# Wait placement and step order redrawn in an attention and state-space kernel on one Trainium2 core

## What is computed

```
# block 1: attention with one head of 128 channels
h = group_norm(x)                                  # 8 groups
q, k, v = split(h @ qkv_w.T + qkv_b)
attn = softmax(q @ k.T / sqrt(128))                # 1024 x 1024 for each image
x = x + (attn @ v) @ proj_w.T + proj_b

# block 2: a selective state-space layer (mamba2) over the 1024 tokens
u = layer_norm(x) * norm_g + norm_b
z, xBC, dt = split(u @ in_w.T);  dt = softplus(dt + dt_bias)
xBC = silu(causal_conv1d(xBC, 4 taps) + conv_b)    # 256 channels: xs 128, B 64, C 64
state = state * exp(dt * A) + dt * xs * B          # 4 heads, from token to token
y = C . state + Dp * xs;  y = rms_norm(y * silu(z)) * rms_w
out = y @ out_w.T
x = x + out * sigmoid(se2(relu(se1(mean_over_tokens(out)))))
```

## Time and profile before

| | us |
|---|---|
| median of 3 runs | 293.25 |
| lowest and highest run | 291.04, 295.36 |
| span of the profiled execution | 289.1 |
| PE busy in it | 262.4 (91%) |
| DVE busy | 238.4 (82%) |
| ACT busy | 210.1 (73%) |
| POOL busy | 113.3 (39%) |

### The profile page before, as it was taken

How to read it: one execution, slowest core, us unless ns; L and a number is a source line. 1 busy time by engine, 2 the same in 40 slices (tenths; PEclk the granted TensorE clock), 3 DMA queues, 4 the chain that set the end, 5 groups by cost and what they waited for, 6 DMA issues and landing times. The chain is left out here.

```text
span 289.1 us, 6193 instructions
## 1 busy us (share of the span) xinstructions
PE 262.4 (91%) x1992; PEld 224.1 (78%) x1992; DVE 238.4 (82%) x517; ACT 210.1 (73%) x414; POOL 113.3 (39%) x114
## 2 busy tenths in 40 slices
PE   3999999999999999989899997899899996999691
PEld 2889978888887788778888696787898885576581
DVE  5795767447869899899999999989998998797933
ACT  2346678968999758859868974877587967888260
POOL 7000043152055201196454172333751166756171
PEclk9999999999999999999999999999999999999995
DMA  5920000040004400000265000330007100000013
GB/s 160 409 101 2 0 2 1 6 144 0 2 0 130 96 0 2 0 2 1 73 161 140 0 2 0 105 83 2 0 6 194 63 1 2 36 0 3 0 39 146
DMA packets 10987, 15.29 MB, mean 53 GB/s; under 512 B 1515, under 2 KB 5708, under 8 KB 10956
## 3 DMA queue, kind: packets, MB, share of 16 engines
q1 hardware_dynamic: 10412, 14.69, 16.3%
q10 hardware_dynamic: 544, 0.21, 0.3%
HBM read 12.70 MB, written 2.20 MB: 52 GB/s over the span
## 5 line engine op out<-in xcount | busy, mean ns | idle before, releaser
L1157 PEld LDWEIGHTS attn_out<-values,pT 128*128 128x128 f32 x512 | 62.1, 191 | 5.8 <-issue 4.5
L1157 PE MATMUL attn_out<-values,pT 128*128 128x129 f32 x512 | 65.5, 275 | 0.3 <-DVE res L985 0.3
L974 DVE TENSOR_REDUCE neg_max<-scores 128x1 f32<-128x1024 f32 x32 | 39.0, 1219 | 11.9 <-PE scores L1157 11.7
L649 ACT ACTIVATE probs<-scores,neg_max 128x512 f32<-128x512 f32 x64 | 41.6, 684 | 9.1 <-DVE neg_max L974 7.8
L655 ACT ACTIVATE pT<-turn 128x512 f32<-128x512 f32 x64 | 37.5, 594 | 11.3 <-PE turn L1230 11.0
L1230 PE MATMUL turn<-ident,probs 128*128 128x128 f32 x256 | 37.4, 274 | 1.7 <-ACT pT L655 1.7
L575 POOL TENSOR_TENSOR pre<-pre,th 128x512 f32<-128x512 f32 x16 | 22.0, 1373 | 42.6 <-ACT pre L681 39.6
L1230 PEld LDWEIGHTS turn<-ident,probs 128*128 128x128 f32 x256 | 29.9, 142 | 5.6 <-issue 3.5
L561 POOL TENSOR_TENSOR ln_rstd<-ln_var,neg_half 128x4 f32<-128x4 f32 x8 | 11.4, 1430 | 55.7 <-DVE ln_var L996 55.6
L1067 DVE TENSOR_TENSOR_SCAN L<-L,ident 128x512 f32<-128x512 f32 x24 | 28.9, 1219 | 0.7 <-DMA L<-decay_rows_d 0.7
L1157 PE MATMUL scores<-h_hi,q_hi 128*128 128x512 f32 x64 | 28.2, 441 | 0.6 <-DVE q_lo L970 0.6
(11 more groups left out here) (219 smaller groups left out, 606.4 us busy)
## 6 DMA issues: line engine op xcount, KB each, us to landing
L<-decay_rows_d SPq DMA_DIRECT2D x24, 256.0 KB, 3.9
res<-in_x_tok SPq DMA_DIRECT2D x4, 512.0 KB, 8.1
out<-res SPq DMA_DIRECT2D x8, 256.0 KB, 2.1
x_all<-in_x SPq DMA_DIRECT2D x3, 512.0 KB, 8.4
decay_in<-decay_rows_d SPq DMA_DIRECT2D x24, 64.0 KB, 3.6
x_all<-in_x SPq DMA_DIRECT2D x2, 256.0 KB, 3.1
winT<-in_in_wT SPq DMA_DIRECT2D x1, 194.0 KB, 6.9
wqkv<-in_qkv_w ACTq DMA_DIRECT2D x1, 192.0 KB, 4.0
```

The source lines that it names most:

```text
L649: act.activation(probs[:, i % 2, half_of(h)], scores[:, half_of(h)], ACT.Exp, bias=neg_max[:, i:i + 1]).then_inc(exp_done.sem, 1)
L974: V.tensor_reduce(neg_max[:, n:n + 1], scores[:, :], AX.X, ALU.max, negate=True).then_inc(max_ready.sem, 1)
L1157: return T.matmul(o, w, v, start=start, stop=stop)
```

## The change

Two things change and nothing else. No instruction is added or taken away on any engine, and the number of EVENT_SEMAPHORE instructions on each engine stays.

First, in the code of some 45 kinds of steps the `wait` calls are written in another order, so that another one of them stands on the instruction. In many cases `take(...)`, which waits for PE's filling of the bank, is now first.

Second, ORDER is a new table, with new bank numbers.

```diff
@@ act: step pT
                     i, h = divmod(n, 2)
+                    bank = take(act, b, "T", n)
                     wait(act, pv_done, b, n - 3)
-                    bank = take(act, b, "T", n)
@@ pool: step g
+                    wait(pool, y_ready, b, n + 1)
                     wait(pool, gate_ready, b, n + 1)
-                    wait(pool, y_ready, b, n + 1)
@@ pe: step S
-                    wait(pe, q_lo_ready, b, i // QUAD + 1)
-                    wait_h_lo(pe, b, h + 1)
                     if i == 0:
                         wait(pe, q_lo_ready, b, h + 1)
                     else:
                         wait(pe, exp_done, b, n - 1)
+                    wait(pe, q_lo_ready, b, i // QUAD + 1)
+                    wait_h_lo(pe, b, h + 1)
@@ pe: step T
+                    wait(pe, exp_done, b, n + 1)
                     pe.wait_ge(vp_ready.sem, 1)
-                    wait(pe, exp_done, b, n + 1)
                     bank, done = fill(pe, b, "T", n)
@@ pe: step PV
+                    if h == 0:
+                        wait(pe, res_ready, b, i)
                     wait(pe, pT_ready, b, n + 1)
                     wait(pe, v_ready, b, h + 1)
-                    if h == 0:
-                        wait(pe, res_ready, b, i)
@@ pe: step UT
+                    wait(pe, u_tok_ready, b, n + 1)
                     pe.wait_ge(win_ready.sem, 1)
                     pe.wait_ge(gn_var_ready.sem, 2)
-                    wait(pe, u_tok_ready, b, n + 1)
@@ ORDER, its first row before and now
-gn_stats0 warm3 gn_mm10 kq_mm gn_dev0 gn_mm20 vp_mm gn_ve0 kq_ev gn_pow0 gn_aff0 h0a h_hi0a h1a h_hi1a h_lo0a h_lo1a
+warm3 gn_stats0 gn_mm10 kq_mm gn_dev0 gn_mm20 kq_ev gn_ve0 vp_mm gn_pow0 gn_aff0 h0a h1a warm5 h_hi0a h_hi1a h_lo0a
```

More of the change, by code:

```diff
@@ new lines @@
+h_lo1a Q0a vp_ev Q1a win_s q_hi0a q_lo0a alog V0a@1 S0a q_hi1a q_lo1a v0a S1a gn_bs1 max0a exp0a xob0b gn_bs2 win_mm
+V1a@0 T0a@1 exp1a S2a v1a xob0a pT0a S3a T1a@0 max1a gn_bs3 pT1a PV0a PV1a exp2a S4a exp3a inv0a T2a@1 S5a res0a pT2a
+stats0a T3a@0 max2a pT3a PV2a exp4a PV3a exp5a S6a T4a@1 pT4a S7a T5a@0 inv1a gn_stats1 res1a gn_mm11 PV4a max3a pT5a
+stats1a win_ev gn_dev1 PV5a exp6a exp7a inv2a S8a res2a T6a@0 S9a max4a T7a@1 pT6a pT7a exp8a PV6a xob1b stats2a PV7a
+T8a@1 inv3a res3a stats3a exp9a S10a pT8a T9a@0 ln_ve0a S11a wo_s PV8a max5a gn_mm21 pT9a gn_ve1 ln_pow0a PV9a gn_pow1
@@ new lines @@
+g1b o0b stats0d XsT0c@0 UT1c@1 PV3d pT5d T6d@0 T7d@1 bc3c u1c Dt1c@2 exp8d sq1b InBC1c@1 xdt0c dt_x1c l3c exp9d
+sp_exp1c os0b pT6d to_end0c xend0c InX1c@0 sp9c fin0a S10d inv1d raw_bc1c Ss1b@2 res1d pT7d sp10c ms1b T8d@1 term3c
+term4c sp11c dd0c raw_x1c S11d sp12c conv_bc4c sp13c sp14c conv_x4c U0c@1 Out1b@2 PV4d st0c G0c@0 y_pow1b sp15c
+stats1d sp16c PV5d max5d o1b sp17c exp10d Cum1c@1 S12d dA1c m0c os1b inv2d dec1c res2d stc0c m1c pT8d conv_bc5c cd1c
+conv_x5c exp11d PV6d term5c DAT1c@2 stats2d PV7d m2c T9d@0 inv3d InZ1c@1 conv_bc6c rows1c conv_bc7c conv_x6c zt1c
@@ L1055, in step @@
                     rows = slice(R * n, R * (n + 1))
+                    bank = take(dve, b, "XsT", n)
                     wait(dve, sp_step, b, SP_STEPS * n + SP_DT)
@@ L1093, in step @@
                     part = slice(P, HALF) if n == 0 else half
+                    bank = take(dve, b, "Yo", n)
                     if by_dma(b):
@@ L1099, in step @@
                     wait(dve, xs_ready, b, n + 1)
-                    bank = take(dve, b, "Yo", n)
                     V.tensor_tensor(yo[:, part], bank[:, P if n == 0 else 0:HALF], decay_in[:, part], ALU.mult
@@ L1117, in step @@
                 elif kind == "y":
+                    bank = take(dve, b, "Y", n)
                     wait(dve, yo_dx_ready, b, n + 1)
@@ L1362, in step @@
                 elif kind == "Pl":
-                    bank, done = fill(pe, b, "Pl", n)
                     if b < BATCH - 1:
@@ L1370, in step @@
                         tiles = [o_tok[:, QUAD * n + k, :] for k in range(QUAD)]
+                    bank, done = fill(pe, b, "Pl", n)
                     for k, t in enumerate(tiles):
```

195 lines of the change are left out of this document (96 added, 99 removed).

## The result

| | before | changed |
|---|---|---|
| median, us | 293.35 (4 runs, 291.0 to 295.4) | 275.91 (4 runs, 275.3 to 276.2) |
| ratio to before, 95% interval | | 0.942 (0.936 to 0.948) |
| span of the profiled execution | 289.1 | 273.1 |
| PE busy | 262.4 (91%) | 256.9 (94%) |
| DVE busy | 238.4 (82%) | 224.8 (82%) |

The kernel is 17.4 us faster. Some executions of a kernel are slower as a whole, at a lower granted clock, so times and ratios from here on are of the fast ones. The prediction was 290.0 us with a range from 284.8 to 295.5, so it was wrong: right in sign, five times too small, and outside its own range. The number that it named as a test of itself is the one that moved most after the span: DVE is shown busy 13.6 us less, with the same instructions.

A forecast was written before the change was run, and what follows sets the result against it. PE was taken to bound until 90 us, DVE until 241 us, then a chain across engines. From the 289.1 us span, 1.9 and 1.5 us off and 0.2 added gave 285.9, hence a median of 290.0 us, range 284.8 to 295.5.

The forecast's parts named there:

- What bounds the kernel: PE bounds from 14.8 to 90 us, DVE by a hair to 241 us, then a chain that hops between engines.
- Part one: Hops whose late wait moves onto the instruction get shorter on PE, ACT and POOL: 1.9 us gained (0.7 to 3.9).
- Part two: The new order covers long stalls, mostly in the DVE-bound stretch: 1.5 us gained, less 0.2 us at the head.
- three stalls that I looked up: Cum1c's 1.19 us wait for `la`, Out1a's 1.44 us for its bank, SP's 0.41 us store issue: 3.0 us.
- the weight of two fifths for PE's time: In the DVE-bound stretch, PE's 2.6 us of removed stalls were counted at two fifths, 1.1 us.
- The head: First 14.8 us: order kept but for three edits; ACT's alog stands in the way of q_lo1a, costing 0.2 us.
- The end: From the last `la` of the attention part on, nine hops from UT1d to the last th_att save 0.7 us.
- the last rival: DVE operations held while POOL works meet it more often, each losing 0.5 to 1.1 us: slower, chance 0.16.
- The waits bite deeper: Shorter hops in the attention loop and half of DVE's idle time closed: 7.7 us gained, about 285 us, chance 0.27.
- Nothing: DVE's work from 90 to 241 us stays, hiding PE's stalls; only the end's 0.7 us gained: 292.5 us, chance 0.15.
- The tests: Signs in the later profile: shorter hops, stalls gone, end 0.7 us shorter, DVE's busy time of 238.4 within 3 us.

The follow-up runs named there:

- before_memset: The kernel before with each large POOL operation replaced by memsets of its target that read no SBUF operand: 279.09 us, ratio 0.957.
- without holding: Large POOL operations replaced by memsets that read no SBUF operand: kernel before 279.1 us, with new waits 278.5, with new table 274.9, changed kernel 273.0.
- the halves: Against the kernel before, each half of the change alone: new wait order with old table 292.59 us (1.000), new table with old wait order 278.85 us (0.954).

## Why the prediction was wrong, step by step

**What bounds the kernel.** Here it failed first. I read "DVE busy 143.4 of 151.0 us" as 143.4 us of work and took 7.6 us as the most that an order could free. The sum had no term for a change in the number of meetings: it stood at nothing. But 17.3 us of these 143.4 were holding (20 of the 29 held operations lie in that stretch), and having fewer of them is worth some 10 us of the 17.4. The mark of it stood in the earlier trace rows, medians and means far from the minimum, and in the earlier trace rows; I used them for a rival only and never summed them over all lines. A sum of 22.6 us would have put the lower bound of the time some 13 us lower, by the price that before_memset gave.

**Part one, the waits, 1.9 us.** The hops behave as forecast. In the changed trace the S steps that waited for exp start 0.05 to 0.06 us behind it (0.11 to 0.12 before); y ends at 223.24 and POOL's g starts 0.07 us later; ln_var ends at 228.90 and POOL starts 0.08 later; u_tok ends at 231.74 and UT1d starts 0.05 later (0.21 before):

```profile
222.56 0.68 DVE L1122 TENSOR_TENSOR y<-mamba,th 128x512 f32<-128x512 f32 x1
223.31 1.27 POOL L588 TENSOR_TENSOR xs<-y,gate 128x512 f32<-128x512 f32 x1
...
230.46 1.28 ACT L662 ACTIVATE u_tok<-res,ln_rstd 128x128 f32<-128x128 f32 x4 [0.39 <-POOL ln_rstd L561]
231.79 0.42 PEld L1248 LDWEIGHTS mamba<-ident,u_tok 128*128 128x128 f32 x4
```

Their worth was 0 with the old table and 2.9 us with the new one (0.6 and 1.9 without holding), around the 1.9 that I wrote. The size of this term was fair, but about 1 us of the 2.9, and 0.7 of the 1.9, may be the pace of the first Q steps and not the waits.

**Part two, the order, 1.5 us.** This term was mis-sized. The table alone gave 13.4 us. The single readings came true: the stalls of Out1a and Cum1c are gone, and so is the wait of a scan of L for its DMA. What failed is (a) that the new table was credited with three stalls that I looked up, one of which was itself made by holding, and (b) the weight of two fifths for PE's time, which stood on the wrong bound. The stalls were also read too long: 1.19 and 1.44 us are idle time of the weight loads, and PE's matmuls stood idle 0.75 and 0.64 us at these places. PE's idle time in the third stretch fell from 9.0 to 1.2 us, and what counts as busy there by another 5.0.

**The head, +0.2 us.** It is 0.2 us shorter. That is less than single executions differ there, so neither size nor sign can be judged.

**The end.** I expected 0.7 us from nine hops, to be seen from the last `la` of the attention part on. That stretch didn't get shorter (48.1 and 48.2 us), so by its own words the test failed. It was badly put: `la` now comes earlier against the attention, and from the last `res` of the attention part to the end it is 2.5 us less (47.6 to 45.1). The chain of the nine hops itself, from UT1d to the last th_att, went from 38.3 to 36.0 us. The waits' part in it is 0.5 us with the old table and 1.1 with the new, 0.9 and 0.5 without holding, so the term of 0.7 us was about right.

**The rivals.** The mechanism that decided is the one that I gave as the last rival, with the right price (0.5 to 1.1 us for each; measured 0.78 on average) and the sentence that eight fewer would equally give 284. It was then entered in the chances with one sign only, 0.16 for slower. Nothing in the profile spoke for more meetings rather than fewer: every meeting's place was drawn anew, and 29 was where the old table stood. It came out at 13 fewer. Two of its figures don't follow from its price: at 0.75 us each, a dozen more would be 299 us and not 295.9, and the upper end of the range, 295.5, stands for seven more and not ten. "The waits bite deeper" (285) had the right direction, for a reason that the halves rule out. "Nothing" (292.5) rested on the same 143.4 us as the forecast.

**The tests.** DVE's busy time was named as the judge, with 3 us as the limit; it moved by 13.6. By this test, which the prediction set itself, it was wrong, and the test pointed at the right mechanism.

The page "SBUF — State Buffer" of the Trainium skill, section "Who interferes with whom", says that a DVE instruction with two SBUF inputs contends with a GpSimd instruction that reads SBUF but not with one that only writes it, while copy, cast and tensor_scalar can contend with GpSimd where they run in a 2-port mode. The runs agree. In the four kernels with memsets, small operations of two SBUF inputs (sp_s, sp_log, dt, la_raw) started 49 times while a memset was on, and none lasted over 0.19 us; in the kernel before, 15 started while POOL was at work and 11 were held, in the changed one 3 of 9. `la` (a tensor_scalar) is still held by a memset:

```profile
80.11 1.11 POOL L540 MEMSET pre<- 128x512 f32 x2
...
80.52 0.16 DVE L873 TENSOR_TENSOR la_raw<-dt,a_neg 128x16 f32<-128x16 f32 x1
80.71 0.54 DVE L875 TENSOR_SCALAR la<-la_raw 128x16 f32<-128x16 f32 x1
```

It ends 0.03 us behind the second memset (80.69 to 81.22), while la_raw, which began 0.12 us before the end of the first, has its plain 0.16 us.

**What stays open.** Taking holding away shows that it is 13 us in one kernel and 3 in the other, but not by which feature the new table avoids it: neither POOL's list nor a few swaps of DVE's did it alone. The 6 us that order and waits together give without holding aren't traced to single steps either. PE's gaps over 0.3 us are nearly the same there (8.8 and 7.5 us); the rest is in gaps of under 0.3 us.
